# One attention layer with a sign-weight feed-forward network: queries stored once and split on GpSimd, one output buffer per head, first head's loads moved behind the last stores

## The reference, cut to what matters

```python
q = split(x @ Wq + bq); k = split(x @ Wk + bk); v = split(x @ Wv + bv)   # b, 16 heads, 2048, 16
q = _rope(q); k = _rope(k)
scores = einsum('bhnd,bhmd->bhnm', q, k) / sqrt(256)
inter = einsum('bhnm,bhmd->bhnd', softmax(scores), v)
attn = inter @ Wo + bo
h = relu(s0 * (concat([x, -x]) @ K0)) * 2     # K0, K1, K2 are +1 / -1
h = relu(s1 * (h @ K1)) * 2
ffn = s2 * (h @ K2)
out = x + attn + ffn
```

## Time and profile before

| | |
|---|---|
| median of 3 runs | 2648.11 us (2647.49 to 2648.26) |
| the profiled execution, its own time | 2645.93 us |
| its span in the trace | 2644.1 us |
| TensorE busy | 2577.4 us, 97% |
| ScalarE busy | 2099.3 us, 79% |
| VectorE busy | 977.5 us, 37% |
| GpSimd busy | 300.0 us, 11% |
| prepare and maxima | from 0 to about 240.8 us |
| attend | from 240.8 us to the end |

### The profile page before, as it was taken

The page is one execution under the profiler, slowest core; times in us unless marked ns, Lnnn a source line. Parts: engine busy times, 40 slices in busy tenths (PEclk is TensorE's granted clock), DMA queues, the critical chain, the costliest instruction groups (busy, mean ns, idle before and its releaser), DMA issues.

```text
span 2644.1 us, 49178 instructions
## 1 busy us (share of the span) xinstructions
PE 2577.4 (97%) x20711; PEld 1340.4 (51%) x20711; DVE 977.5 (37%) x1665; ACT 2099.3 (79%) x2342; POOL 300.0 (11%) x268
## 2 busy tenths in 40 slices
PE   7886999999999999999999999999999999999999
PEld 5663454444445454545445454544445454544545
DVE  7773323343324233243324233243324233242323
ACT  6885888888888878788887878788887878788884
POOL 6783000000000000000000000000000000000000
PEclk9997999999999999999999999999999999999999
DMA  9995111111212112121212212121212212121212
GB/s 283 294 292 171 37 47 52 53 61 49 57 43 75 51 48 71 50 77 53 78 44 70 63 46 70 53 77 51 77 43 67 61 53 69 57 77 49 77 38 97
DMA packets 202199, 210.45 MB, mean 80 GB/s; under 512 B 144685, under 2 KB 148605, under 8 KB 195577
## 3 DMA queue, kind: packets, MB, share of 16 engines
q1 hardware_dynamic: 199672, 198.91, 25.1%
q10 hardware_dynamic: 2304, 8.39, 0.9%
HBM read 131.34 MB, written 75.89 MB: 78 GB/s over the span
## 4 chain that ended last, share of the span: by engine, by line
PE 91%; ACT 0%; DVE 0%; issue 0%; DVEq 0%; SPq 0%
PE ps_o L1042 37%; PE ps_f L1075 27%; PE ps_s L1029 24%; PE ps_y L1088 2%; PE ps_s L1124 0%; PE ps_f L1124 0%; ACT probs L1009 0%; DVE probs L1266 0%; PE ps_f L1132 0%; PE ps_o L1124 0%; PE ps_y L1124 0%; PE ps_s L1132 0%; DVEq L819 0%; PE ps_o L1132 0%; PE ps_y L1132 0%
## 5 line engine op out<-in xcount | busy, mean ns | idle before, releaser
L1009 ACT ACTIVATE probs<-ps_s 128x1024 f32<-128x1024 f32 x2048 | 1930.0, 1034 | 453.1 <-PE ps_s L1029 450.7
L1042 PE MATMUL ps_o<-probs,v_ones 128*32 128x512 f32 x8192 | 1011.3, 600 | 0.0
L1029 PE MATMUL ps_s<-q_rows,k_rows 50*128 50x512 f32 x4096 | 868.9, 439 | 5.1 <-SPq L981 4.1
L1029 PEld LDWEIGHTS ps_s<-q_rows,k_rows 50*128 50x128 f32 x4096 | 365.7, 184 | 672.2 <-ACT probs L1009 600.3
L1042 PEld LDWEIGHTS ps_o<-probs,v_ones 128*32 128x32 f32 x8192 | 200.6, 108 | 418.3 <-issue 295.8
L1075 PE MATMUL ps_f<-h_hi,ffn_w 64*128 64x512 f32 x2048 | 410.2, 393 | 0.0
L1075 PE MATMUL ps_f<-h_lo,ffn_w 64*128 64x512 f32 x2048 | 409.3, 391 | 0.0
L1209 DVE COPY raw<-ps_f 128x512 f32<-128x512 f32 x256 | 164.9, 686 | 560.4 <-PE ps_f L1075 560.4
L1164 POOL TENSOR_TENSOR heads<-heads,sums 128x512 f32<-128x512 f32 x64 | 82.3, 1285 | 2149.8 <-DVE sums L1185 2149.8
L1185 DVE RECIPROCAL sums<-sums 128x128 f32<-128x128 f32 x256 | 226.6, 924 | 1.7
L1075 PEld LDWEIGHTS ps_f<-h_lo,ffn_w 64*128 64x128 f32 x2048 | 198.7, 186 | 34.2
(11 more groups left out here) (118 smaller groups left out, 1384.6 us busy)
## 6 DMA issues: line engine op xcount, KB each, us to landing
k_rows<-k_parts SPq DMA_DIRECT2D x128, 256.0 KB
q_rows<-q_parts SPq DMA_DIRECT2D x384, 64.0 KB
q_parts<-parts SPq DMA_DIRECT2D x32, 512.0 KB, 8.7
k_parts<-parts SPq DMA_DIRECT2D x32, 512.0 KB, 8.3
k_rows<-k_parts SPq DMA_DIRECT2D x128, 128.0 KB
x_chunk<-in_x ACTq DMA_DIRECT2D x16, 512.0 KB, 7.3
xn_d<-xn_t SPq DMA_DIRECT2D x16, 512.0 KB, 8.6
v_heads<-v_sb SPq DMA_DIRECT2D x16, 512.0 KB, 7.7
```

The lines of the kernel that those rows point to most:

```text
L1009: nc.scalar.activation(probs[:, s % PBUF, half * 2 * C:(half + 1) * 2 * C], ps_s[:, half].rearrange("p c n -> p (c n)"), ACT.Exp, scale=SC ...
L1029: last = nc.tensor.matmul(ps_s[:, half, w], k_rows[rows, u, t * P:(t + 1) * P], q_rows[rows, u, half], start=True, stop=True)
L1042: last = nc.tensor.matmul(ps_o[32 * c:32 * c + 2 * DH], v_ones[:, u, t], probs[:, s % PBUF, c * C:(c + 1) * C], start=(t == 0), stop=(t == ...
```

## The change

- Queries are stored to DRAM once, as they are (`q_heads`, two tiles of one part in place of two of two parts). In `prepare` GpSimd writes the turned queries straight to their store buffer (two buffers for each tile); ScalarE's copy and GpSimd's subtraction are made for the keys only.
- In `attend` all three groups of 16 query rows are loaded with the same values, and GpSimd makes the low part in the third group (`split_queries`): a copy of the whole 128x1024 tile to `q_hi` (rounded), a multiplication with `lo_rows` (1 in the rows of the third group, 0 elsewhere), and a subtraction. The scores of a head wait for `q_split` in place of `rows_loaded`. For head 0 the same three instructions stand in `prepare`, after chunk 8.
- `heads` and `sums` have one buffer. `finish` waits until the head before is stored. SyncE's loop over j is as it was.
- Head 0's queries are loaded before chunk 7's stores, its keys and the first `xn` chunk behind the last stores. The stores of the shift go to ScalarE's queue. `Wo`, `bv` and `bo` are loaded together.
- `d0` lies in `q_hi`; `maxima` splits its queries on VectorE.

```diff
         def store_parts(n):
-            sp.wait_ge(parts_ready, n + 1)
-            to = q_out[b, j, COLUMNS[r]] if j < 2 else k_out[b, j % 2, r]
-            sp.dma_start(to, parts[:, u].bitcast(F32)).then_inc(parts_stored[u], 16)
+            if j < 2:
+                sp.wait_ge(turn_done, n + 1)
+                sp.dma_start(q_out[b, j, COLUMNS[r]], parts[:, j, c % 2].bitcast(F32)).then_inc(parts_stored[j], 16)
+            else:
+                sp.wait_ge(parts_ready, 2 * c + j - 1)
+                sp.dma_start(k_out[b, j - 2, r], parts[:, j].bitcast(F32)).then_inc(parts_stored[j], 16)
...
+            load_first_keys()
             sp.wait_ge(fill_ready, 2)
...
+            act.wait_ge(fill_ready, 2)
+            store_shift(act, 0, bound_fill, bound_stored)
...
+                if c == FIRST_QUERIES_AT + 1:
+                    pool.wait_ge(first_loaded, 16 * 6)
+                    nc.gpsimd.tensor_copy(w["q_hi"][:].bitcast(F32R), first_q.bitcast(F32)).then_inc(first_q_high, 1)
...
                 if t == 0 and half == 0:
-                    pe.wait_ge(rows_loaded[u], 16 * LOADS * 2 * i + 16 * LOADS * (j // 2 + 1))
+                    if HEADS * i + j > 0:
+                        pe.wait_ge(q_split, HEADS * i + j)
...
+            def split_queries(g):
+                at = q_rows[:, g % 2].rearrange("p h n -> p (h n)")
+                pool.wait_ge(rows_loaded[g % 2], 16 * LOADS * (g // 2 + 1))
+                nc.gpsimd.tensor_copy(q_hi[:].bitcast(F32R), at.bitcast(F32)).then_inc(q_step, 1)
...
+                nc.gpsimd.tensor_tensor(q_hi[:], q_hi[:], lo_rows[:, 0:1].broadcast_to([P, 2 * C]), ALU.mult).then_inc(q_step, 1)
...
+                nc.gpsimd.tensor_tensor(at, at.bitcast(F32), q_hi[:], ALU.subtract).then_inc(q_split, 1)
...
                     pool.wait_ge(sums_inverted, PIECES * HEADS * i + PIECES * (j + 1))
-                    nc.gpsimd.tensor_tensor(heads[:, u], heads[:, u], sums[:, u], ALU.mult).then_inc(heads_ready, 1)
+                    nc.gpsimd.tensor_tensor(heads[:], heads[:], sums[:], ALU.mult).then_inc(heads_ready, 1)
+                    if i < PASSES - 1 or j < HEADS - 2:
+                        split_queries(HEADS * i + j + 2)
...
             def finish(i, j):
-                u = j % 2
-                dve.wait_ge(heads_stored[u], 32 * CB * i + 16 * CB * (j // 2 + 1))
+                for u in range(2):
+                    dve.wait_ge(heads_stored[u], 16 * CB * ((HEADS * i + j + 1 - u) // 2 + 1))
+                    dve.sem_inc(tail_begun, 1)
+                if HEADS * i + j > 0:
+                    dve.wait_ge(heads_ready, HEADS * i + j)
+                    dve.sem_inc(tail_begun, 1)
                 dve.wait_ge(pv_done, STEPS * i + (KT * (j + 1) + PBUF))
-                nc.vector.tensor_copy(heads[:, u], ps_o[:]).then_inc(raw_ready, 1)
+                nc.vector.tensor_copy(heads[:], ps_o[:]).then_inc(raw_ready, 1)
```

More of the change, by code:

```diff
@@ L266, in prepare, with store_shift @@
         block = ctx.enter_context(nc.Block())
+        def store_shift(queue, a, filled, landed):
+            to = scratch["shift"][a].rearrange("g (h w n) -> w (g h) n", h=P // G, n=FILL)
+            for n in range(G * N // (P * FILL)):
+                queue.dma_start(to[n], filled.bitcast(F32)).then_inc(landed, 16)
         def here(c):
@@ L272, in _ @@
         def _(sp):
[L273 to L276, removed]
             sp.dma_start(ident[:], a["ident"]).then_inc(ident_loaded, 16)
@@ L353, in _ @@
                 sp.wait_ge(v_stored[u], 16 * (NC // 2))
-            for u in range(PART_BUFS):
-                sp.wait_ge(parts_stored[u], 16 * (4 * NC // PART_BUFS))
+            for j in range(PART_BUFS):
+                sp.wait_ge(parts_stored[j], 16 * NC)
         @block.scalar
@@ L545, in _, with low @@
             nc.gpsimd.tensor_tensor(wv_lo[:], wv[:], wv_hi[:].bitcast(F32), ALU.subtract).then_inc(w_split, 1)
[L547 to L553, removed]
-                pool.wait_ge(products_ready, n + 1)
[L555 to L560, removed]
+            def low(m):
+                j = 2 + m % 2
+                pool.wait_ge(part_high, m + 1)
+                nc.gpsimd.tensor_tensor(parts[:, j, 1], turned[:, m % 3], parts[:, j, 0].bitcast(F32), ALU.subtract).then_inc(parts_ready, 1)
@@ new lines, in turn @@
+            def turn(n):
+                c, j, u = n // 4, n % 4, n % 2
+                pool.wait_ge(products_ready, n + 1)
+                m = 2 * c + j - 2
+                if j >= 2:
+                    to = turned[:, m % 3]
+                    if m >= 3:
+                        pool.wait_ge(parts_ready, m - 2)
+                else:
+                    to = parts[:, j, c % 2].bitcast(F32)
+                    if c >= 2:
+                        pool.wait_ge(square_ready, 4 * (c - 2) + j + 1)
+                        pool.wait_ge(parts_stored[j], 16 * (c - 1))
+                nc.gpsimd.tensor_tensor(to, by_cos[:, u], by_sin[:, u], ALU.add if n % 2 else ALU.subtract).then_inc(turn_done, 1)
@@ L561, in _ @@
+            for c in range(NC):
+                turn(4 * c)
+                if c > 0:
+                    low(2 * c - 1)
+                turn(4 * c + 1)
+                turn(4 * c + 2)
+                turn(4 * c + 3)
+                low(2 * c)
+                if c == FFN_WEIGHTS_AT:
                     pool.wait_ge(d0_ready, 1)
                     nc.gpsimd.memset(w["v_ones"][:, :, :, DH:2 * DH], 1.0)
-            low(4 * NC - 1)
+                if c == FIRST_QUERIES_AT + 1:
+                    pool.wait_ge(first_loaded, 16 * 6)
+                    nc.gpsimd.tensor_copy(w["q_hi"][:].bitcast(F32R), first_q.bitcast(F32)).then_inc(first_q_high, 1)
+                    pool.wait_ge(first_q_high, 1)
+                    nc.gpsimd.tensor_tensor(w["q_hi"][:], w["q_hi"][:], w["lo_rows"][:, 0:1].broadcast_to([P, 2 * C]), ALU.mult).then_inc(first_q_high, 1)
+                    pool.wait_ge(first_q_high, 2)
+                    nc.gpsimd.tensor_tensor(first_q, first_q.bitcast(F32), w["q_hi"][:], ALU.subtract)
@@ L661, in _ @@
             nc.vector.memset(fill[:].bitcast(F32), 0.0).then_inc(zero_ready, 1)
-            dve.wait_ge(tables_loaded, 32)
+            dve.wait_ge(tables_loaded, 48)
+            nc.vector.tensor_scalar(w["minus_lo"][:], w["lo_rows"][:], -1.0, None, ALU.mult)
             for c in range(NC):
@@ L780, in _ @@
                 with dve.Fori(0, G) as g:
+                    dve.wait_ge(rows_loaded, 16 * 5 * g + 16 * 5)
+                    nc.vector.tensor_copy(q_hi[:].bitcast(F32R), q_rows[:].bitcast(F32)).then_inc(q_high, 1)
+                    dve.wait_ge(q_high, g + 1)
+                    nc.vector.scalar_tensor_tensor(out=q_rows[:], in0=q_hi[:], scalar=w["minus_lo"][0:AUG, 0:1], in1=q_rows[:].bitcast(F32),
+                                                   op0=ALU.mult, op1=ALU.add).then_inc(q_split, 1)
                     for t in range(KT):
@@ L794, in heads_of, with load_keys, load_queries @@
     return (scratch[name].rearrange("am (g e) n -> g am e n", e=HALF) for name in ("k", "q"))
-def load_rows(sp, scratch, g, q_rows, k_rows, loaded, only=None):
+def load_keys(queue, scratch, g, k_rows, loaded):
     k_head, q_head = heads_of(scratch)
-    shift = scratch["shift"].rearrange("a g (w n) -> g w a n", w=2)
+    for w in range(2):
+        at = GROUP_ROWS * w
+        queue.dma_start(k_rows[at:at + 2 * DH, :].bitcast(F32), k_head[g]).then_inc(loaded, 16)
+        queue.dma_start(k_rows[at + 2 * DH:at + AUG, :].bitcast(F32), k_head[g, 0:2]).then_inc(loaded, 16)
+def load_queries(queue, scratch, g, q_rows, loaded):
+    k_head, q_head = heads_of(scratch)
     q_flat = q_rows.rearrange("p h n -> p (h n)")
@@ L804, in load_rows, with load_shift @@
         here = slice(w * N // 2, (w + 1) * N // 2)
[L805 to L812, removed]
+        queue.dma_start(q_flat[at:at + DH].bitcast(F32), q_head[g, 0:2, :, here]).then_inc(loaded, 16)
+        queue.dma_start(q_flat[at + DH:at + 2 * DH].bitcast(F32), q_head[g, 0:2, :, here]).then_inc(loaded, 16)
+        queue.dma_start(q_flat[at + 2 * DH:at + AUG].bitcast(F32), q_head[g, 0:2, :, here]).then_inc(loaded, 16)
+def load_shift(queue, scratch, g, q_rows, loaded):
+    shift = scratch["shift"].rearrange("a g (w n) -> g w a n", w=2)
+    q_flat = q_rows.rearrange("p h n -> p (h n)")
+    for w in range(2):
+        at = GROUP_ROWS * w + AUG
+        queue.dma_start(q_flat[at:at + PARTS].bitcast(F32), shift[g, w]).then_inc(loaded, 16)
 def attend(nc, a, w, scratch, out, bound_stored):
@@ L829, in attend @@
         probs = sb("probs", [P, PBUF, N], F32)
-        heads = sb("heads", [P, 2, C], F32)
-        sums = sb("sums", [P, 2, C], F32)
+        heads = sb("heads", [P, C], F32)
+        sums = sb("sums", [P, C], F32)
+        q_hi, lo_rows = w["q_hi"], w["lo_rows"]
         raw = sb("raw", [P, 2, C], F32)
@@ L1131, in last_head @@
                         at, n = slice(32 * r, 32 * r + DH), t % 2
```

(2 more changed lines are left out.)

106 lines of the change are left out of this document (64 added, 42 removed).

## The result

The changed kernel takes 3483.11 us, median of 4 runs (3480.26 to 3483.78), against 2647.8 us before (median of 4 runs, one more than in the table above). The ratio is 1.3154, interval 1.3139 to 1.3170. The forecast was 3450 us, its range 3380 to 3545.

The account below looks back on a forecast made before the run. Attend was taken as bound by TensorE (busy 2577 of 2644 us), prepare by DMA. 2645.9 + 759 (waits) + 60 (clock) + 0 (split) - 17 (prepare) = 3448 us, forecast as 3450; range 3380 to 3545 us.

Parts of the forecast that it names:

- The place and the number of the waits: In attend, TensorE waits before `weigh` at the end of heads 1, 2, 3, none at head 0: 46 waits.
- The price of a wait: At a head's end in attend: copy 18.7 us later, less 2.2 slack, plus 0.1 hand-over: 16.5 us each, 759 in all.
- four slow loads: In SyncE's queue in attend: four value loads, 10.24 us to issue, stand ahead of the previous head's four stores.
- The bound that took 2.4 us off: Lower bound in attend: without the first store's slow issue behind the value loads, 14.1 us a wait, 649 us.
- Rival D: In attend, the chain of loads and stores shortens to about half: about 370 us of waits, 3050 us; chance 0.02.
- The clock: After each attend wait TensorE runs 4 us at half clock, losing 2 us; net 1.3 us each, 60 us.
- ScalarE's lead: After each attend wait, ScalarE has worked off all scores, so TensorE's small waits for it go: 0.7 us back.
- `split_queries`: Three GpSimd instructions of 2.45 us, 7.3 us a head, hidden in attend: cost 0, by 4 us.
- Prepare: The stage before attend, bound by DMA, gets 17 us shorter; bounds -28 and -5.
- The period of the first chunks: In prepare, 12.8 us a chunk falls to 11.5: 14 us saved over 11, less 3 us for head 0's split.
- The last four chunks: In prepare they take 55.9 us, with head 0's loads in between; 7 us were to be saved.
- 4.3 us at 302 GB/s: At prepare's end, keys and `xn` (1.25 MB) behind the last store drain in that time; 1 us cost taken.

Follow-up runs that it names:

- run 1: The changed kernel, but SyncE stores head j-1 before it waits for the end of head j's scores: 2634.86 us, ratio 0.9957.
- run 2: The kernel before the change, with only the single `heads` and `sums` buffers and the new waits of `finish`: 3495.8 us, ratio 1.3213.
- run 4: The changed kernel, but the store of head j-1 is issued between the row loads and value loads of head j+2: 3398.48 us.
- run 5: The changed kernel with its late stores, but each head's query rows and key rows together in DRAM, outermost dimension 16 or 32: 2909.66 us, ratio 1.0996.
- run 6: The changed kernel with each head's rows together in DRAM and the store of head j-1 before the wait for head j's scores: 2627.55 us, ratio 0.9931.

## Why the prediction was right

*The place and the number of the waits* were right: 46, at the end of heads 1, 2 and 3, none at head 0. Runs 1 and 2 show that they, with the half clock behind them, are the whole effect.

*The price of a wait* was put at 16.5 us and measured as 743.8 / 46 = 16.2: 744 us and not 759. (The prediction's own terms, 18.7 - 2.2 + 0.1, give 16.6 and not 16.5.) Why that chain is so long it did not ask. The prediction took the value loads' 10.24 us as their own length, "four slow loads". Runs 4 and 5 show that these loads, and the stores behind them, wait for the row loads ahead, which by the DMA share and the layout's effect lie on few DMA engines. That did not move the number, since the change leaves the chain as it was, but it misses what would have to be mended. The bound that took 2.4 us off for the first store's slow issue named the same backlog without seeing its source. Rival D, a chain that shortens by itself, fell: the value loads take 9.87 us after as well. Its time is 3450 - 759 + 370 = 3061 us by its own terms, and not 3050.

*The clock* is the term that was mis-sized: 1.3 us a wait, 60 us, where 2.2 us, 100 us, were measured by keeping TensorE busy. TensorE's busy time says the same: 2677.6 us against 2573.4 us in run 1, 104.2 us more for the same matmuls. In the changed kernel's trace the clock stays at 0.50 for 3.3 to 5.9 us behind the 46 waits, 4.8 us on average (5.7 in the one shown above), and not the 4 us read in the earlier trace rows: that is 2.4 us of work a wait and not 2. Of the 0.7 us that were given back for ScalarE's lead no more than some 0.2 us came, the distance from 2.4 to 2.2.

*`split_queries`* is hidden, by more than forecast. The rounding copy takes 1.04 us and the multiplication 1.89, where 2.45 were assumed for each. At the tightest place:

```profile
1057.67 1.29 POOL L1235 TENSOR_TENSOR heads<-heads,sums 128x512 f32<-128x512 f32 x1 [52.39 <-DVE sums L1263]
1058.90 1.04 POOL L1217 CAST q_hi<-q_rows 128x1024 fp32r<-128x1024 f32 x1
1060.12 1.89 POOL L1220 TENSOR_TENSOR q_hi<-q_hi,lo_rows 128x1024 f32<-128x1024 f32 x1 [0.18 <-POOL q_hi L1217]
1062.19 2.38 POOL L1223 TENSOR_TENSOR q_rows<-q_rows,q_hi 128x1024 fp32r<-128x1024 f32 x1 [0.18 <-POOL q_hi L1220]
```

It ends at 1064.6, and the next head's scores begin at 1070.8, 6.2 us later, the smallest distance of all 63 splits. GpSimd is busy for 632.9 us, not the 700 forecast. Beside that subtraction VectorE has to stand, and ends 0.55 us after it:

```profile
1062.33 2.79 DVE L1298 SCALAR_TENSOR_TENSOR h_lo<-raw,h_hi 128x512 fp32r<-128x512 f32 x1
```

That is 2.79 us for 0.69. By the rule of the Trainium skill (SBUF — State Buffer, "Who interferes with whom"), that a VectorE instruction with two SBUF inputs and a GpSimd instruction that reads SBUF exclude one another, this had to come; here the trace agrees. VectorE's `h_lo` takes 846 ns on average where it took 693, and attend's 2404.2 us in run 1 show that nobody waits for it.

*Prepare* was forecast at -17 us and gave -11.7, from terms that were each off; that they came out so near is luck. The period of the first chunks fell from 12.8 to (167.87 - 33.14) / 11 = 12.2 us: 6 us, where 14 less 3 for the split of head 0 were forecast. The last four chunks fell from 55.9 to 38.5 us, 17 us and not 7. Head 0's query loads moved from the latter stretch to the former; how much of the two misses that explains was not measured. The end lost 11.7 us and not 1: from the last key store to attend it was 240.7 - 229.7 = 11.0 us and is now 229.0 - 206.3 = 22.7. The step that failed there is "4.3 us at 302 GB/s": the keys are row loads and drain on few engines. They are issued by 211.5 us, and the DMA share is 0.27 at 216 us, 0.13 at 222 and 0.00 only from 226 us on. With the rows together (run 6) the end takes 221.05 - 204.79 = 16.3 us: 6.4 of the 11.7 us are the few engines, and the rest stays where the keys stand behind the last stores.

The end of prepare in the changed kernel:

```profile
206.34 1.68 SPq L310 DMA_DIRECT2D k_parts<-parts  x2
...
210.85 0.63 SPq L843 DMA_DIRECT2D k_rows<-k_parts  x1
...
229.02 0.75 SPq L842 DMA_DIRECT2D k_rows<-k_parts  x1
```

*The sum*: 2645.9 + 743.8 + 100 - 11.7 + 5 (open) = 3483. The forecast's sum of 3448 is short by 35 us: 40 of the clock, 5 of prepare and 5 open, less 15 of the waits. That the shorter waits took 15 us off a miss of 50 is luck too: nothing ties the two.

## What to carry to other kernels

Before you give up a buffer, look at where the instruction that frees it stands in its queue: data that are ready early free nothing as long as their store is issued behind a wait for something later. Here moving one call turned a ratio of 1.315 into 0.996. Where a chain of DMAs is long, ask what it waits for before you take its length as given: a DMA share that stays at 2 of 16 while issues pile up means few engines, and the outermost dimension of the loads ahead is the place to mend it.

## What the runs showed of the hardware that was not expected

- Row loads at a DMA share of 2 in 16 held up what was issued behind them on the same queue. A 32 KB store issued behind them landed after 12.9 us in place of 1.7, and SyncE took 9.8 to 11.0 us to issue four value loads in the changed kernel. With the rows together in DRAM it took 2.0 us (median) for the same four.
- The time to issue a row load fell as well, from about 0.61 to 0.42 us, with the single block.
- GpSimd at 128x1024 in fp32: a rounding copy 1.04 us, a multiplication with a broadcast column 1.89 us, a subtraction of two full tiles 2.39 us.
- A VectorE instruction of 0.69 us lasted 2.79 us beside a GpSimd subtraction, with the wait inside its shown length and not before it.
- Behind the 46 stops of some 16 us the granted clock was at 0.50 for 3.3 to 5.9 us of work, 4.8 us on average; behind the 46 stops of 4.2 us of run 5 for 4.0 us on average. In the run with 67 matmuls in each wait, with stops of at most 1.8 us, it stayed at 1.00.
